# A four-tap convolution moved from matmuls to DVE and ACT, and a softplus series without a division, in the Mamba inputs of a graph network stack

## The reference

```python
xz = xs @ in_proj_w.T
xc, z = jnp.split(xz, 2, axis=-1)
K = conv_w.shape[1]                                  # 4 taps
xp = jnp.pad(xc, ((K - 1, 0), (0, 0)))
xc = sum((xp[k:k + n] * conv_w[:, k] for k in range(K))) + conv_b
xc = jax.nn.silu(xc)
dbc = xc @ x_proj_w.T
dt = jax.nn.softplus(dbc[:, :DT_RANK] @ dt_proj_w.T + dt_proj_b)
...
dBx = (dt * xc)[:, :, None] * Bm[:, None, :]
```

## Time and profile before

| | |
|---|---|
| median of 3 runs | 9494.0 us (9464.22 to 9521.39) |
| profiled execution | 9492.08 us, span 9490.2 us |
| PE busy | 6016.9 us (63%) |
| DVE busy | 5517.9 us (58%) |
| POOL busy | 4461.2 us (47%) |
| ACT busy | 3116.3 us (33%) |
| mean granted PE clock | 0.793 |

### The profile page before, as it was taken

The page is one execution under the profiler, slowest core; times in us unless marked ns, Lnnn a source line. Parts: engine busy times, 40 slices in busy tenths (PEclk is TensorE's granted clock), DMA queues, the critical chain, the costliest instruction groups (busy, mean ns, idle before and its releaser), DMA issues. The chain is left out here.

```text
span 9490.2 us, 107605 instructions
## 1 busy us (share of the span) xinstructions
PE 6016.9 (63%) x19722; PEld 3676.1 (39%) x19722; DVE 5517.9 (58%) x11195; ACT 3116.3 (33%) x10661; POOL 4461.2 (47%) x4386
## 2 busy tenths in 40 slices
PE   5488526888888844656777775574565564556555
PEld 4333203444444422223444443463344443334333
DVE  8353775778888753557888895562344443323322
ACT  1001004666666521337777785340000000000000
POOL 0122004555555424007777774324655654666564
PEclk9877758989999865778888897796677776677777
DMA  2114206767677654236667666222333335333334
GB/s 74 30 62 185 73 17 207 223 216 227 218 226 221 189 190 124 70 100 215 234 239 244 237 236 166 68 67 78 101 113 111 115 112 89 93 112 116 108 112 84
DMA packets 483045, 1352.07 MB, mean 142 GB/s; under 512 B 128663, under 2 KB 223035, under 8 KB 482074
## 3 DMA queue, kind: packets, MB, share of 16 engines
q0 software_dynamic: 238272, 838.09, 30.5%
q1 hardware_dynamic: 210156, 443.65, 13.8%
q10 hardware_dynamic: 34316, 67.14, 2.1%
HBM read 1133.35 MB, written 546.45 MB: 177 GB/s over the span
## 5 line engine op out<-in xcount | busy, mean ns | idle before, releaser
L1159 POOL DMA_INDIRECT rows_e<-bundle,unit_src x1856 | 1763.0, 950 | 1187.4 <-issue 486.7
L1180 PE MATMUL acc_e<-rows_e,hot_e 128*128 128x256 f32 x3712 | 1271.3, 494 | 1055.2 <-issue 493.9
L577 POOL DMA_INDIRECT rows_e<-table,unit_src x928 | 1009.5, 1088 | 1322.0 <-PE acc_e L765 601.4
L936 POOL DMA_INDIRECT rows_e<-table,unit_src x928 | 1140.5, 1229 | 871.3 <-POOLq L234 430.5
L765 PE MATMUL acc_e<-rows_e,hot_e 128*128 128x512 f32 (+1 forms) x3712 | 1400.2, 534 | 202.1 <-DVE sums_e L789 116.0
L1180 PEld LDWEIGHTS acc_e<-rows_e,hot_e 128*128 128x128 f32 x3712 | 849.9, 246 | 1445.6 <-issue 1043.7
L754 ACT ACTIVATE rows_e<-rows_e 128x64 f32<-128x64 f32 x4640 | 1119.0, 334 | 3.7
L1189 DVE SCALAR_TENSOR_TENSOR sums_e<-sums_e,unit_keep,acc_e 128x256 f32<-128x256 f32 x928 | 443.7, 478 | 1110.1 <-remote 658.9
L765 PEld LDWEIGHTS acc_e<-rows_e,hot_e 128*128 128x128 f32 x3712 | 736.8, 204 | 798.4 <-issue 674.4
L1022 ACT ACTIVATE rows_e<-rows_e 128x64 f32<-128x64 f32 x3712 | 922.6, 333 | 27.3 <-issue 14.0
L2252 ACT ACTIVATE turned_f<-turn_f 128x512 f32<-128x512 f32 x98 | 58.5, 597 | 2290.3 <-DMA given_f<-bundle 1610.0
(11 more groups left out here) (445 smaller groups left out, 9100.7 us busy)
## 6 DMA issues: line engine op xcount, KB each, us to landing
bc<-bc_rows SPq DMA_DIRECT2D x226, 896.0 KB
summed<-sums_e SPq DMA_DIRECT2D x464, 390.0 KB
bundle<-sums_e SPq DMA_DIRECT2D x928, 128.0 KB
summed<-sums_e SPq DMA_DIRECT2D x464, 130.5 KB
given_f<-bundle ACTq DMA_DIRECT2D x98, 384.0 KB
rows_e<-table,unit_src POOLq DMA_INDIRECT x1856
rows_e<-bundle,unit_src POOLq DMA_INDIRECT x1856
summed<-zeros POOLq DMA_DIRECT2D x50, 390.0 KB, 22.7
```

The lines of the kernel that those rows point to most:

```text
L577: pool.indirect_dma_start(self.rows[:, v, e, :], None, table, bass.IndirectOffsetOnAxis(unit_src[:, u, e:e + 1], 0)).then_inc(self.landed[ ...
L936: pool.indirect_dma_start(self.rows[:, v, e, :], None, self.tab, bass.IndirectOffsetOnAxis(unit_src[:, u, e:e + 1], 0)).then_inc(self.land ...
L1159: pool.indirect_dma_start(self.rows[:, v, e, :], None, self.tab, bass.IndirectOffsetOnAxis(unit_src[:, u, e:e + 1], 0)).then_inc(self.land ...
L1180: mm = pe.matmul(self.acc[:, v % 2, 0:D], self.hot[:, v % self.SUMS, e, :], self.rows[:, v, e, :], start=(e == 0), stop=(e == 1))
```

## The change

The convolution leaves PE. ACT writes tap 0's product for both channel groups into `dtx`, DVE adds taps 1 to 3 in place with one scalar_tensor_tensor for each group and tap, ACT applies Silu. The `taps` tile and its eight products go. In softplus, log(1 + u) with u = exp(-|x|) was a series in u / (u + 2) with a reciprocal; it is now a polynomial of degree 9 in u. max(x, 0) moves from DVE to ACT (Relu), into the step of Exp. A half now has 39 steps, and track k begins at turn 10 k.

```diff
-                taps = isb("taps", [P, 2, 4, P])
...
-                chain.apart(*[(dve, lambda c=c, k=k: dve.tensor_scalar(taps[:, c, k, :], ident[:, :], cw[:, c, k:k + 1], None,
-                                                                       ALU.mult)) for c in range(2) for k in range(4)])
...
-                    for c in range(2):
-                        yield ch.step(pe, *[lambda n=n: pe.matmul(ps, taps[:, c, n, :], xin[:, k, c, n:n + HS],
-                                                                  start=(n == 0), stop=(n == 3)) for n in range(4)])
-                        yield ch.step(act, lambda: act.activation(xc[:, k, c, :], ps, ACT.Silu, bias=cb[:, c:c + 1]))
+                    yield ch.step(act, *[lambda c=c: act.activation(dtx[:, k, c, :], xin[:, k, c, 0:HS], ACT.Copy, scale=cw[:, c, 0:1])
+                                         for c in range(2)])
+                    for n in range(1, 4):
+                        yield ch.step(dve, *[lambda c=c: dve.scalar_tensor_tensor(
+                            dtx[:, k, c, :], xin[:, k, c, n:n + HS], cw[:, c, n:n + 1], dtx[:, k, c, :], ALU.mult, ALU.add)
+                            for c in range(2)])
+                    yield ch.step(act, *[lambda c=c: act.activation(xc[:, k, c, :], dtx[:, k, c, :], ACT.Silu, bias=cb[:, c:c + 1])
+                                         for c in range(2)])
...
                     yield ch.step(act, lambda: act.activation(u, d_, ACT.Abs))
-                    yield ch.step(act, lambda: act.activation(u, u, ACT.Exp, scale=-1.0))
-                    yield ch.step(dve, lambda: dve.tensor_scalar(q, u, 2.0, None, ALU.add))
-                    yield ch.step(dve, lambda: dve.reciprocal(q, q))
-                    yield ch.step(dve, lambda: dve.tensor_tensor(u, u, q, ALU.mult))
-                    yield ch.step(act, lambda: act.activation(q, u, ACT.Square))
-                    yield ch.step(dve, lambda: dve.tensor_scalar(dx, q, 1.0 / 13, None, ALU.mult))
-                    for n in (11, 9, 7, 5, 3):
-                        yield ch.step(dve, lambda: dve.scalar_tensor_tensor(dx, dx, 1.0 / n, q, ALU.add, ALU.mult))
-                    yield ch.step(dve, lambda: dve.scalar_tensor_tensor(dx, dx, 1.0, u, ALU.add, ALU.mult))
-                    yield ch.step(dve, lambda: dve.tensor_scalar(d_, d_, 0.0, None, ALU.max))
-                    yield ch.step(dve, lambda: dve.scalar_tensor_tensor(d_, dx, 2.0, d_, ALU.mult, ALU.add))
+                    yield ch.step(act, lambda: act.activation(u, u, ACT.Exp, scale=-1.0),
+                                  lambda: act.activation(d_, d_, ACT.Relu))
+                    yield ch.step(dve, lambda: dve.tensor_scalar(dx, u, LOG1P[-1], None, ALU.mult))
+                    for n in LOG1P[-2::-1]:
+                        yield ch.step(dve, lambda: dve.scalar_tensor_tensor(dx, dx, n, u, ALU.add, ALU.mult))
+                    yield ch.step(dve, lambda: dve.tensor_tensor(d_, dx, d_, ALU.add))
                     yield ch.step(dve, lambda: dve.tensor_tensor(dx, d_, xc[:, k, :, :], ALU.mult))
...
-                        if track[k] is None or turn < 11 * k:
+                        if track[k] is None or turn < 10 * k:
```

More of the change, by code:

```diff
@@ L57 @@
 RING = 16
+LOG1P = (0.9999999698794722, -0.49999493139350404, 0.3331909678405794, -0.24842982026917387, 0.19106006030265443,
+         -0.13663244241678296, 0.07822593357169284, -0.029505227536289626, 0.005232691459110232)
 NOT_POOL = (ENG.Activation, ENG.PE, ENG.DVE, ENG.SP)
@@ L1817, in prep @@
                         yield ch.step(act, lambda: act.activation(dt[:, k, c, :], ps, ACT.Identity, bias=db[:, c:c + 1]))
-                    u, q, dx, d_ = (v[:, k, :, :] for v in (u_, xT, dtx, dt))
+                    u, dx, d_ = (v[:, k, :, :] for v in (u_, dtx, dt))
                     yield ch.step(act, lambda: act.activation(u, d_, ACT.Abs))
-                    yield ch.step(act, lambda: act.activation(u, u, ACT.Exp, scale=-1.0))
-                    yield ch.step(dve, lambda: dve.tensor_scalar(q, u, 2.0, None, ALU.add))
-                    yield ch.step(dve, lambda: dve.reciprocal(q, q))
-                    yield ch.step(dve, lambda: dve.tensor_tensor(u, u, q, ALU.mult))
-                    yield ch.step(act, lambda: act.activation(q, u, ACT.Square))
-                    yield ch.step(dve, lambda: dve.tensor_scalar(dx, q, 1.0 / 13, None, ALU.mult))
-                    for n in (11, 9, 7, 5, 3):
-                        yield ch.step(dve, lambda: dve.scalar_tensor_tensor(dx, dx, 1.0 / n, q, ALU.add, ALU.mult))
-                    yield ch.step(dve, lambda: dve.scalar_tensor_tensor(dx, dx, 1.0, u, ALU.add, ALU.mult))
-                    yield ch.step(dve, lambda: dve.tensor_scalar(d_, d_, 0.0, None, ALU.max))
-                    yield ch.step(dve, lambda: dve.scalar_tensor_tensor(d_, dx, 2.0, d_, ALU.mult, ALU.add))
+                    yield ch.step(act, lambda: act.activation(u, u, ACT.Exp, scale=-1.0),
[4 more added lines that the diff above has]
+                    yield ch.step(dve, lambda: dve.tensor_tensor(d_, dx, d_, ALU.add))
                     yield ch.step(dve, lambda: dve.tensor_tensor(dx, d_, xc[:, k, :, :], ALU.mult))
```

## The result

The changed kernel takes 9415.6 us (median of 7 runs, 9371.6 to 9450.8) against 9494.6 us for the kernel before: ratio 0.9925, interval 0.9901 to 0.9948. Two later measurements gave 0.9918 (0.9889 to 0.9947) and 0.9918 (0.9892 to 0.9943). The profiled execution took 9438.0 us.

What follows compares the result with a forecast made beforehand. No engine is full, so the order of waits decides: load, PE steps, then DVE rows ahead of the finishing track. Ten intervals -45, beginning -8, end -6, set-up -2 make -61 us: about 9433 against the median, range 9390 to 9472.

Steps and rivals of the forecast that it cites:

- The ten intervals: Half 0's end to half 10's: 275.3 us instead of 322.9, 47.6 less; 3 given back for `spread_own`, so -45.
- Track 1 to 2: Interval between these tracks' half ends: 11.5 + 6.95 + 0.65 + 1.1, then 8.2 on DVE, 28.4 us.
- Start and end: Half 0 gains 8 us from shorter DVE work; the last three halves take about 44 instead of 49.6, -6.
- The set-up: Eight `taps` products ahead of the first load go: at most 3.3 us, put at -2.
- The convolution pair: Two 448-wide scalar_tensor_tensor rows on DVE: 0.61 us each by a straight line, about 1.25 with semaphore.
- The uncertainty of ±2.5 us per half: DVE's six 448-wide convolution rows per half: 0.61 us each was taken, with ends of 0.41 and 1.09.
- PE's load: PE's busy time per half after the change: about 15 us, from 311.6 - 104.8 over 14.
- PE waits in total more for `xg_t`: Sign of being right: PE's total load wait grows from 101.9 us, since less is queued ahead.
- The clock rival: PE, with less work, stays at 1.2 GHz more: some 10 us lost, gain 50, 9444 us; chance 0.15.
- DVE's collisions: Pairs serialize two tracks, 2 to 3 us more per interval: gain 30 to 40, 9455 to 9464; chance 0.19.
- Relu: Maximum moved to ACT: 0.95 us late against 0.63 saved; by the skill's rule 4 us lost in all.
- The slower rival: Ten extra ACT and DVE rows during POOL's scatters and gathers cost some 11 us each: 9543 us; chance 0.04.

Runs made afterwards that it cites:

- unused products: Changed kernel with the old convolution products put back on PE, their result overwritten: ratio to before 0.9929, tens 261.3 us; again 0.9938, tens 259.3 us.
- series alone: Kernel before with only the new softplus, convolution still on PE, tracks beginning at turn 10 k: ratio 0.9893, tens 230.8 us; again 0.9870, tens 218.6 us.
- the fold: max(x, 0) folded into DVE's last sum, run with the load ahead of the stores: ratio 0.9842 with convolution on PE, 0.9813 with it split.
- the early load: Changed kernel with each track's next load issued once its transposes are through, ahead of the stores: ratio to before 0.9815, tens 191.1 us.
- the first four experiments: Runs of a quicker series, including the new softplus alone and the unused convolution products on PE; the kernel before took 8901.5 us there.

## Why the prediction came out

- *The time.* 9433 was forecast, 9390 to 9472 as range, 9415.6 came: a gain of 79 us (49 to 94) where the sum had 61; in the traces the stage itself gained 67.7, and the rest of the 79 is within the interval. The mechanism was read correctly: the interval hangs on the load, then on the PE steps behind it, then on what stands ahead of the last products on DVE.
- *The ten intervals.* 275.3 plus 3 was forecast, 273.0, 273.6 and 269.5 measured. By kinds, from SP's rows of the first trace: 29.9, 28.1, 27.8 (27.9 forecast); 25.6, 29.2, 25.8 (28.4); 26.9, 32.1 (29.2); 23.5, 24.1 (24.0). Track 1 to 2 was laid out some 1.5 us too long, the others within 0.7 in the mean.
- *Start and end.* -8 forecast, -12.3 and -5.6 measured in two pairs of traces; -6 forecast, -5.4 and -7.1 measured. The set-up's -2 cannot be told: the stage began 11 us later than before in the first pair of traces and 39 us earlier in the second.
- *Sizes.* The convolution pair was put at 1.25 and takes 1.27 to 1.28. ACT's copies were put at 1.1 a pair by the row of an eviction and take 1.22. Both are in these rows, groups by line of the changed kernel:

```profile
L1810 DVE SCALAR_TENSOR_TENSOR dtx<-xin,cw,dtx 128x448 f32<-128x448 f32 x84 | 53.7, 681 | 143.1 <-ACT dtx L1807 143.0
...
L1807 ACT ACTIVATE dtx<-xin,cw 128x448 f32<-128x448 f32 x28 | 17.0, 658 | 0.0
```

One row of 448 is 681 ns, not 610, but two without a wait between overlap. The uncertainty of ±2.5 us per half does not follow from the ends that it names: six rows at 0.41 or 1.09 instead of 0.61 are -1.2 or +2.9. PE's load was put at about 15 us per half and is 17.2 (240.8 over 14), as the sum took the old rows at their old clock. Of the 143.0 us that DVE idles ahead of the pairs, 98.4 lie in the tens, about 10 an interval: the wait that the prediction laid out.
- *Signs that did not hold.* "PE waits in total more for `xg_t`": it waits 91.7 us, less than the 101.9 of the earlier trace rows. In-projections above 0.75 us were named as a sign of being wrong; they average 0.816 in the first trace, and the time held all the same, because the sum had the exposed ones at the low clock's price already. Two more signs of being wrong came. L1829 and L1830 do wait long behind pairs (polynomial done at 4087.2, L1829 at 4098.6); but the prediction's own layout has that wait, so it could not tell right from wrong. And the first half ended at 3854.7, later than 3850; from the first load it took 98.9 us instead of 111.3, and only the later start of the stage put it there.
- *The clock rival.* It gave 10 us more than the sum and a gain of 50. Its condition came in part: the clock of the tens was 0.73 (0.78 before) and the in-projections 816 ns (700). The unused products show the size, some 10 us in the tens, but the sum already contained it. The Trainium skill's rule in "TensorE: Matmul & The Clock Gate", section "HAM oscillation — how this bites in real kernels", that short bursts between DMA waits start at half rate each time, agrees with these traces: 3.22 us behind a wait of 6.56, 1.68 behind one of 0.60.
- *DVE's collisions.* The rival with 2 to 3 us more per interval did not come; what it described, two tracks tied together that were not before, is in the sum at the size laid out.
- *What the sum did not ask.* It took the change as one and so did not see that its halves pull against each other. Of the tens, the series takes 90 to 104 us off; the convolution adds 9 to 11 alone, and 39 to 55 on top of the series (16 to 28 when the tracks begin at turn 11 k), by letting PE fall to the low clock in the load's wait, by rows of its own on DVE, and by putting pairs ahead of the finishing track. It gives back about 8 us at each end. In the stage, from the first load to the last half's stores, that is 411.5 us for the change and 377.2 for the series alone on one chip: moving the convolution lost 34 us there. It was not the work taken off PE that lost them, for with those products back, unused, the stage is longer still (425.1); it was what came in their place on DVE and ACT.
- *Relu.* It was not tried alone; the fold ran only together with the early load, so what it is worth stays open.
- *The slower rival.* ACT idled 10.66 us ahead of single rows in the first stretch here too, and the stretch to half 0's end got shorter, not longer. It did not come.

## What to carry to other kernels

Where engines run a fixed interleaving of several tracks and none is full, an interval is set by what stands ahead of the finishing track's last rows and of the next load's first reader, not by busy sums; write down those rows for each track position before costing anything. Work that stands inside a wait costs nothing there, so taking it away gains nothing there either (7 us of unused products per half left the tens 10 us shorter, and the two ends of the stage, which have no such wait, 24 us longer). Try each half of a change alone, and take the wait away (the load ahead of the stores gave some 80 us of the tens, the whole change 50) before moving the work that fills it. How far apart the tracks begin is worth a run of its own when the number of steps changes: 11 instead of 10 turns took 23 to 27 us off the tens.

## What the runs showed of the hardware

The runs fell in series that differ. In the others the kernel before takes 9481 to 9495 us; in that of the first four experiments it takes 8901.5. The record gives the same chip number for this quicker series and for one of the others, so whether the chip or something else made the difference stays open. In this stage the tens hardly differ (unused products 261.3 and 259.3; series alone 230.8 and 218.6, and the whole of that difference is one interval, half 1 to half 2, of 31.4 and 19.3 us). But the first stretch does, while POOL gathers and scatters: in the others ACT idles 8 to 13 us at a time, in three traces once 21 to 32, and what the trace names as the end of the wait does not explain it (nothing, or a load that landed long before), as here in the changed kernel. In the traces of the quicker series there is no such stall.

```profile
3800.21 0.54 ACT L1798 ACTIVATE xin<-mm_ps_t 128x448 f32<-128x448 f32 x1 [8.87 <-DMA xg_t<-sorted_h]
3811.41 0.54 ACT L1817 ACTIVATE dbc<-mm_ps_t 48x448 f32<-48x448 f32 x1 [10.66 <-issue]
3822.61 0.54 ACT L1798 ACTIVATE zs<-mm_ps_t 128x448 f32<-128x448 f32 x1 [10.66 <-DMA xg_t<-sorted_h]
```

These rows come 11.2 us apart. To half 0's end the series-only kernel takes 58.2 us in the quicker series and 105.9 in another, the unused products 71.6 and 110.9. What the stalls are was not tried; a kernel whose POOL begins later would tell whether they follow its gathers and scatters.
